# A token tile's twelve score products in one group at the head of its step

## What is computed

```python
x = x + xattn(layernorm(x), ctx)          # q = ln(x) @ wq.T + bq; k, v from ctx
#   scores = einsum('bhqd,bhkd->bhqk', q, k) / sqrt(16)
#   attn = softmax(scores); values = attn @ v; out = values @ wo.T + bo
x = x + moe(layernorm(x))
#   scores = softmax(x @ wg); top 2 of 8 experts, with a capacity per expert
#   h = silu(x_e @ fc1_w.T + fc1_b); y = h @ fc2_w + fc2_b; weighted sum
#   layernorm of (input + sum) * gamma + beta
```

## Time and profile before

| what | value |
|---|---|
| median of 3 runs | 857.68 us (853.38 to 858.8) |
| the profiled execution | 853.83 us, of which the span of its instructions is 851.7 us |
| PE, PEld, DVE, ACT, POOL busy | 701.4, 663.6, 588.3, 387.1, 452.6 us |
| mean granted TensorE clock | 0.903 of full speed |

### The profile page before, as it was taken

One profiled execution on the slowest core, in us unless ns is written; L12 is line 12 of the kernel. 1 busy time (PEld: TensorE's weight loads), 2 busy tenths in 40 slices (PEclk: granted clock), 3 DMA queues, 4 the chain that ended last, 5 costly groups with the idle time before them and its releaser, 6 DMA issues.

```text
span 851.7 us, 17101 instructions
## 1 busy us (share of the span) xinstructions
PE 701.4 (82%) x5635; PEld 663.6 (78%) x5637; DVE 588.3 (69%) x1145; ACT 387.1 (45%) x859; POOL 452.6 (53%) x498
## 2 busy tenths in 40 slices
PE   4599999999999812499999996999979999999100
PEld 2578999889998702399999996999979999999100
DVE  3878788887887599365565667677666666843296
ACT  1235555555555422244454555455554455633142
POOL 3615536455363245635445556758557464622497
PEclk9579999999999955599999997999999999999655
DMA  9301011100111141113424445345344342422553
GB/s 295 117 1 39 26 38 38 38 32 32 38 38 38 38 154 13 48 43 88 95 45 101 101 101 104 54 102 114 93 100 103 51 98 45 63 28 26 134 175 111
DMA packets 55438, 63.84 MB, mean 75 GB/s; under 512 B 9408, under 2 KB 50624, under 8 KB 55232
## 3 DMA queue, kind: packets, MB, share of 16 engines
q0 software_dynamic: 15360, 21.31, 15.7%
q1 hardware_dynamic: 34896, 40.96, 14.5%
q10 hardware_dynamic: 5104, 0.44, 0.5%
HBM read 38.96 MB, written 23.72 MB: 74 GB/s over the span
## 4 chain that ended last, share of the span: by engine, by line
PE 77%; DVE 7%; POOL 6%; issue 5%; DMA 2%; ACT 1%; POOLq 0%; SPq 0%; DVEq 0%; ACTq 0%
PE banks L738 17%; PE banks L739 17%; PE banks L740 17%; PE banks L849 9%; PE banks L836 5%; PE banks L824 5%; POOL z L559 3%; PE banks L946 2%; PE banks L902 2%; POOL oh_id L525 2%; DMA sum_rows<-y_sb,slot_ids 1%; PE banks L862 1%; DMA wv_sb<-in_wvT 1%; PE banks L772 1%; PE banks L892 1%
## 5 line engine op out<-in xcount | busy, mean ns | idle before, releaser
L503 POOL DMA_INDIRECT sum_rows<-y_sb,slot_ids x80 | 134.4, 1680 | 181.7 <-ACT y_sb L697 145.9
L708 ACT ACTIVATE hraw<-banks,b_now 128x256 f32<-128x256 f32 x320 | 132.1, 474 | 104.3 <-PE banks L740 95.6
L738 PE MATMUL banks<-xT_hi,w_hi 128*128 128x256 f32 x560 | 163.5, 292 | 0.0
L739 PE MATMUL banks<-xT_lo,w_hi 128*128 128x256 f32 x560 | 160.8, 287 | 3.1 <-issue 3.1
L740 PE MATMUL banks<-xT_hi,w_lo 128*128 128x256 f32 x560 | 160.4, 286 | 0.0
L738 PE MATMUL banks<-w_hi,h_hi 128*128 128x256 f32 x528 | 149.1, 282 | 2.8 <-issue 2.8
L739 PE MATMUL banks<-w_lo,h_hi 128*128 128x256 f32 x528 | 148.8, 282 | 0.0
L740 PE MATMUL banks<-w_hi,h_lo 128*128 128x256 f32 x528 | 148.7, 282 | 0.0
L1333 DVE TENSOR_TENSOR h_lo<-hraw,h_hi 128x512 fp32r<-128x512 f32 x160 | 116.0, 725 | 5.5
L1331 DVE CAST h_hi<-hraw 128x512 fp32r<-128x512 f32 x160 | 73.2, 458 | 64.8 <-ACT hraw L708 64.6
L739 PEld LDWEIGHTS banks<-xT_lo,w_hi 128*128 128x128 f32 x560 | 108.4, 194 | 3.6 <-issue 3.6
(11 more groups left out here) (183 smaller groups left out, 1468.7 us busy)
## 6 DMA issues: line engine op xcount, KB each, us to landing
w1raw<-in_w1T SPq DMA_DIRECT2D x8, 1024.0 KB
w2raw<-in_w SPq DMA_DIRECT2D x8, 1024.0 KB
xn_rows<-xn SPq DMA_DIRECT2D x32, 128.0 KB, 1.7
sum_rows<-xn SPq DMA_DIRECT2D x32, 128.0 KB, 1.8
res<-sum_rows SPq DMA_DIRECT2D x16, 256.0 KB, 3.1
out<-z SPq DMA_DIRECT2D x16, 256.0 KB, 2.1
X<-in_x SPq DMA_DIRECT2D x2, 1280.0 KB, 13.6
xg<-xn_rows,slot_ids POOLq DMA_INDIRECT x80
```

The lines of the kernel that those rows point to most:

```text
L503: g.indirect_dma_start(sum_rows, bass.IndirectOffsetOnAxis(ap=slot_ids[:, st, 1, q:q + 1], axis=0), y_sb[:, u, q, :], None, bounds_check=N ...
L708: a.activation(hraw[:, j // 2, j % 2, :], banks[:, j // 2, (j % 2) * 256:(j % 2 + 1) * 256], ACT.Silu, bias=b1_now[:, (c // SPE) % 2, j:j ...
L738: t_.matmul(o, a_hi, b_hi, start=first, stop=False)
L739: t_.matmul(o, a_hi, b_lo, start=False, stop=False)
```

## The change

In `step(i, u)` of the PE program the call `scores(1)` moves up, directly behind `scores(0)`. Before, it stood behind the first group of transposed probabilities and the value transposes. Nothing else is edited.

```diff
@@ -853,6 +853,7 @@
                             m.then_inc(sem("pv_done"), 1)
 
                 scores(0)
+                scores(1)
                 transpose_probs(0)
                 if within(t - 2, NT):
 
@@ -861,7 +862,6 @@
                     for c in range(DC):
                         m = t_.transpose(banks[:, TR, c * P:(c + 1) * P], vals[:, c * P:(c + 1) * P], ident[:])
                     m.then_inc(sem("valsT_done"), 1)
-                scores(1)
                 transpose_probs(1)
                 weigh_values(0)
                 if within(i + 1, PAIRS):
```

## The result

The changed kernel takes 863.05 us (median of 5 runs, 861.11 to 866.39), against 856.56 us for the kernel before in the same set of runs (5 runs, 853.38 to 858.80). The ratio is 1.0081, with a 95% interval of 1.0047 to 1.0116: a small loss, 6.5 us, just short of 1%. Forecast were 865.8 us and a ratio of 1.009. The forecast started from a median of 857.68 us of three runs; with five the median before is 1.1 us lower, so by the difference it was 1.6 us too high (8.1 us against 6.5).

The account below looks back on a forecast made before the run. PE was taken to bound the attention stage; 0.34 us saved at drains against a longer copy wait made steps 0.30 us longer, 28 times 8.4 us, minus 0.3 at tile 3: 857.7 + 8.1 = 865.8 us, range 860 to 871.

Parts of the forecast that it names:

- The bound: Attention stage from 70 us: PE sets the pace, busy 120.00 of 120.00 us; steps take 7.08 and 8.18 us.
- The saved part: Head of each step: joining the score groups saves 0.29 + 0.05 = 0.34 us a step.
- the fourth pair: Score pair starting on a new bank with other weights: 0.14 us taken, 0.25 us the other end.
- The lost part: Group 1 waits for ACT's copy of group 0: 0.58 + 0.49 + 0.14 = 1.21 us, starting 0.32 us later.
- What else moves: Value transposes, ACT's later copies, DVE's shift and SP's DMAs: they move with PE or stay hidden, costing nothing.
- Rival A: Step head: drains decide, the copy does not; gain of 0.34 us a step, 848.2 us; chance 0.07.
- B: Attention steps: PE's 0.3 us are absorbed because another engine holds the step; time stays 857.7 us; chance 0.06.
- C: 70 to 270 us: clock falls to 1.2 GHz for a tenth of PE's work, 20 us more, 886 us; chance 0.07.
- How often: Tiles 4 to 31: 28 steps at 0.30 us each, 8.4 us; tile 3 wins 0.3 us, sum +8.1 us.
- Tiles 1 and 2: Early steps mostly at the 1.2 GHz level: signs differ, nothing taken, 0.5 us either way for each.
- Tile 3's step: Scores move ahead of value transposes waiting for DVE: at most 0.38 us won once, 0.3 us taken.
- the split of the chances: Whole kernel: slower 0.42, within 1% 0.51, faster 0.07; the forecast's own 0.80 split 0.45 within 1%, 0.35 slower.

Follow-up runs that it names:

- the pair of runs above (joined and broken): Joined: changed kernel with group 0 transposed a step early, group 2 before next rows or queries, 846.70 us; broken: same, second score group behind group 1, 855.78 us.
- the one with the smaller copy: Changed kernel with transpose groups 0 and 1 of half 0 cut as 2 + 3 pieces instead of 3 + 2: 861.03 us, ratio 1.0077 to the kernel before.
- the first experiment: Kernel before with the second score group moved behind group 1 of the transposed probabilities, score products still in two groups: 876.35 us, ratio 1.026.

## Why the prediction was right

**The bound.** PE set the pace of the stage, and what PE waited for came on top of the step: steps grew by 0.31 and 0.30 us where 0.30 was forecast (7.08 to 7.39, 8.18 to 8.48).

**The saved part** was right: the fourth pair costs 0.14 us, the value taken and not the upper end of 0.25; and the pair of runs above (joined and broken) gives 0.34 us at the head of an even step.

**The lost part** was right in each of its three terms, 0.58, 0.49 and 0.14 us, and group 1 started at 2.26 us where 2.25 was forecast. The price of the restart, read from a single place of the old trace (tile 1), held in all 28 steps (0.14 to 0.15 us).

**What else moves** was right where it said nothing would: DVE and ACT kept up, and the clock stayed at 1.00 between 70 and 280 us. One sign did not come: DVE's wait at the reciprocal was to be longer by 0.3 us a step. Between 70 and 290 us it is 14.1 us in 28 cases, against 15.2 us in 29 before. The stall lies in the middle of PE's step, and DVE meets it earlier in its own: it waits 17.1 us instead of 14.2 at the queries' lower parts (line 1074), and in 12 cases instead of 2 at the residual (line 1175). The sum does not rest on this sign. Rival A (drains alone, 848 us) fell to the result itself, B (absorbed) to the step lengths, C (clock) to the granted clock.

**How often** was right in the number of steps. The stall of tile 31's step, and the head of that step:

```profile
286.91 0.41 PE L824 MATMUL banks<-KH_hi,q_hi 64*128 64x308 f32 x2
...
289.18 0.41 PE L836 MATMUL banks<-ident,probs 128*124 128x128 f32 x2 [0.45 <-ACT probsT L621]
```

It took 6.92 us to the next step's first transposes (293.83), against 6.62 us before (279.63 to 286.25). So all 28 steps grew by 0.30 us, 8.40 us in all. The rest, counted along the two profiles:

- **The start.** The first score product of tile 0 stands at 26.62 us instead of 26.98, although up to there both programs do the same. In the eight profiles of this document it stands between 26.62 and 27.48 us, so these 0.36 us are scatter and not a gain.
- **Tiles 1 and 2** together came out 0.13 us shorter. The forecast had put nothing, and that was luck: it left 0.5 us open for each, and both lie far outside. Tile 1's step took 16.39 us (40.01 to 56.40) instead of 14.66 us (40.38 to 55.04), and tile 2's 7.82 us (56.40 to 64.22) instead of 9.68 us (55.04 to 64.72). The clock had more part in it than the stalls for a copy (0.67 and 0.24 us in the changed kernel). Between 44.9 and 47.8 us the granted clock was 0.50 (the 1.2 GHz level) in the changed kernel and 1.00 before, and the query products there took 1.2 us longer. Between 58 and 62 us it was 0.80 against 0.50. In the five other kernels with a stall of 0.57 to 0.67 us near 43 us, in tile 1, the stretch from 44.9 to 47.8 us had 0.50 to 0.58, and in the one with group 0 ahead of the scores, which has no such stall, 0.72. So the stall may have put off the rise, but with one profile of each kernel this is not shown.
- **Tile 3's step** took 9.39 us (64.22 to 73.61) instead of 9.71 us (64.72 to 74.43): 0.32 us won, where 0.3 was forecast.
- **Behind tile 31's step** the changed kernel's profile is 0.28 us shorter (565.17 against 565.45 us). I have no cause for that, and profiles differ by more there: behind the head of tile 31 both kernels take 572.1 us, and the one with the smaller copy takes 573.95 us.

Together: 8.40 - 0.36 - 0.13 - 0.32 - 0.28 = 7.31 us, the difference of the two spans. The steps and tile 3 give 8.1 us, as forecast. For the three other terms the profiles show no cause in the change. The medians differ by 6.5 us, which their scatter of 5 us allows. That the measured ratio falls within 1% and not beyond was close, as the split of the chances had said.

## What to carry to other kernels

A group of instructions that stands between a producer and the wait for its copy is a cover. Before such a group is moved to save a mode change, read how much of it is cover: here 0.61 us of products hid a wait of which 0.45 us came to light, and the change saved 0.34 us. After the first wait is covered, look for the next one in line (here DVE's shift, with 0.37 us to spare), for the gain ends there until that is covered too. The price of a wait that a trace does not show can be read from a single place where the same pair of engines did wait.

## What the runs showed of the hardware

Products on 64 of the 128 rows cost extra at each change to and from full height, and the extra depends on what follows: a transpose behind a score group is slowed at its first one (0.27 us for two, against 0.22 us), while six weigh_values behind one took 0.80 us instead of 0.70. The second I had not expected. It shows in the first experiment (163.57 to 164.37).

The score products differ from their neighbours in more than the rows: they take inputs rounded to fp32r, and they are 308 columns wide. The number format is not what costs. The products with wo (lines 738 to 740) take fp32r inputs too, at full height. Three transposes and the first of those products take 157.00 - 156.54 = 0.46 us in the changed kernel, which is three transposes of 0.11 us and one product of 0.12 to 0.13 us, with nothing on top. Nor do changes of width among the full-height instructions: from the 256 columns of these products to the 136 of weigh_values it is 0.12 us (157.47 to 157.59). So the height is what is left. But no run has 308 columns at full height, and a cost of that width is not ruled out.

With one group of twelve instead of two of six, an even step's head was 0.34 us shorter with no other difference between the kernels (1.53 against 1.87 us).

The restart of PE behind ACT's copy took 0.14 us in all places where it was read: at tile 1 of the kernel before, in the changed kernel (155.02 to 155.16, and before group 3 of an odd step 166.36 to 166.50) and with the smaller copy (154.63 to 154.78, 0.15 us).
